# Flamingo block, 64 batches on one core: the move of the scaled rows into the float32r tile goes in two transfers instead of one

## The reference

```python
q = layernorm(x) @ W.T + b
p = softmax(q @ ctx.T + (1 - mask) * -1e9)
x = x + tanh(g_xattn) * (p @ ctx)
x = x + tanh(g_ffn) * (layernorm(x) @ sign(weight).T)
```

## Time and profile before

| | |
|---|---|
| median of three runs | 277.24 us |
| the profiled execution | 277.72 us |
| its span in the trace | 275.9 us |
| TensorE matmul busy | 269.5 us, 98% of the span |
| TensorE weight load busy | 259.0 us |
| VectorE busy | 243.7 us |
| ScalarE busy | 239.7 us |
| GpSimd busy | 178.9 us |
| granted TensorE clock | 1.00 |
| moved by DMA | 64.51 MB in 62754 packets |

### The profile page before, as it was taken

The page is one execution under the profiler, slowest core; times in us unless marked ns, Lnnn a source line. Parts: engine busy times, 40 slices in busy tenths (PEclk is TensorE's granted clock), DMA queues, the critical chain, the costliest instruction groups (busy, mean ns, idle before and its releaser), DMA issues.

```text
span 275.9 us, 9092 instructions
## 1 busy us (share of the span) xinstructions
PE 269.5 (98%) x2215; PEld 259.0 (94%) x2215; DVE 243.7 (88%) x756; ACT 239.7 (87%) x708; POOL 178.9 (65%) x462
## 2 busy tenths in 40 slices
PE   7999999999999999999999999999999999999994
PEld 6899999999999999999999999999999999999983
DVE  2799989999999999999999999999999999998694
ACT  3579899899999999999999999999999999999752
POOL 2387676676677667667666766766676676666553
PEclk9999999999999999999999999999999999999999
DMA  5984797878788787878878877777877877775322
GB/s 147 287 204 122 229 278 236 259 237 284 232 272 255 246 267 241 263 243 266 259 238 274 245 252 254 261 257 233 280 243 249 262 259 251 235 254 175 114 78 114
DMA packets 62754, 64.51 MB, mean 234 GB/s; under 512 B 25425, under 2 KB 38801, under 8 KB 62737
## 3 DMA queue, kind: packets, MB, share of 16 engines
q1 hardware_dynamic: 62016, 63.79, 74.2%
q10 hardware_dynamic: 720, 0.53, 0.7%
HBM read 32.31 MB, written 16.78 MB: 178 GB/s over the span
## 4 chain that ended last, share of the span: by engine, by line
PE 91%; DMA 3%; POOL 1%; ACT 1%; DVE 1%; issue 1%; SPq 1%; POOLq 0%; ACTq 0%
PE ffn_ps L891 21%; PE pv_ps L884 19%; PE l_ps L946 16%; PE ctx_ps L811 11%; PE x1t_ps L952 10%; PE xt_ps L838 6%; PE pt_ps L875 6%; DMA x_in<-in_x_dram 3%; POOL rstd L330 1%; DVE st L597 0%; PE xt_ps L841 0%; PE l_ps L986 0%; DVE xs L617 0%; POOLq L45 0%; SPq L235 0%
## 5 line engine op out<-in xcount | busy, mean ns | idle before, releaser
L946 PE MATMUL l_ps<-m_sb,x_t 128*128 128x77 f32 x488 | 74.1, 254 | 0.1
L946 PEld LDWEIGHTS l_ps<-m_sb,x_t 128*128 128x128 f32 x488 | 71.5, 191 | 0.3 <-issue 0.3
L330 POOL TENSOR_TENSOR rstd<-ve,minus_half 128x4 f32<-128x4 f32 (+1 forms) x70 | 67.4, 963 | 5.5
L952 PE MATMUL x1t_ps<-ident,x 128*128 128x128 f32 x244 | 66.5, 273 | 0.0
L884 PE MATMUL pv_ps<-ctx_v,p_t 77*128 77x256 f32 x252 | 64.8, 379 | 0.0
L448 ACT ACTIVATE xs<-x_in,shift,rstd 128x256 f32<-128x256 f32 x118 | 63.8, 591 | 0.0
L326 POOL TENSOR_TENSOR ve<-st,eps 128x4 f32<-128x4 f32 (+1 forms) x70 | 14.1, 201 | 73.5 <-DVE st L597 73.3
L678 DVE SCALAR_TENSOR_TENSOR x<-pv_ps,recip,x_in 128x256 f32<-128x256 f32 x126 | 54.6, 475 | 0.4 <-PE pv_ps L884 0.3
L597 DVE BATCH_NORM_STATS2 st<-x_in 128x6 f32<-128x512 f32 x64 | 44.0, 687 | 5.3 <-DMA x_in<-in_x_dram 5.3
L386 POOL TENSOR_TENSOR y<-ffn_scaled,x 128x256 f32<-128x256 f32 x63 | 46.3, 735 | 3.2 <-ACT ffn_scaled L515 2.0
L597 DVE BATCH_NORM_STATS2 st<-x 128x6 f32<-128x512 f32 x64 | 43.9, 686 | 3.2
(11 more groups left out here) (100 smaller groups left out, 440.0 us busy)
## 6 DMA issues: line engine op xcount, KB each, us to landing
x_in<-in_x_dram SPq DMA_DIRECT2D x64, 256.0 KB, 2.8
out_dram<-y SPq DMA_DIRECT2D x63, 256.0 KB, 2.4
xs_r<-xs SPq DMA_DIRECT2D x58, 256.0 KB, 2.3
ctx_v<-in_ctx_dram SPq DMA_DIRECT2D x32, 154.0 KB
mask_in<-in_mask_BxSxS_ik_dram SPq DMA_DIRECT2D x32, 154.0 KB, 2.9
ctx_sq<-in_ctx_dram SPq DMA_DIRECT2D x120, 40.0 KB, 2.6
wq_raw<-in_L_xattn_W_dram ACTq DMA_DIRECT2D x1, 256.0 KB, 4.2
wf_raw<-in_L_ffn_weight_dram SPq DMA_DIRECT2D x1, 256.0 KB, 8.4
```

What stands on the lines that cost most here:

```text
L330: pool.tensor_tensor(rstd[:, i, kinds], ve[:, i, kinds], minus_half[:, kinds], ALU.pow).then_inc(rstd_done, 1)
L946: ins = pe.matmul(l_ps[:, j * K:(j + 1) * K], x_t[:, r % 2, c, j * P:(j + 1) * P], m_sb[:, c, r % R], start=(c == 0), stop=(c == C - 1))
L952: ins = pe.transpose(x1t_ps[:, c, j * P:(j + 1) * P], x1[:, (r - 2) % R, j, c * P:(c + 1) * P], ident[:])
```

## The change

`move_xs` issues two DMAs in place of one: row j = 0 of every partition behind `xs0_done`, then row j = 1 behind `xs1_done`. Each copies 1 KB in each of the 128 partitions. Both raise the same semaphore by 16, so the value that TensorE waits for grows by 32 from one use of a buffer to the next, and `moved` says so.

```diff
         def moved(t0, n):
 
-            return t0 * (DMA // 2) + DMA * ((n - MOVE_FIRST) // 2 + 1)
+            return t0 * DMA + T * DMA * ((n - MOVE_FIRST) // 2 + 1)
...
                 i = n % 2
 
-                sp.wait_ge(xs0_done, t0 + n + 1)
-                sp.wait_ge(xs1_done, t0 + n + 1)
-                sp.dma_start(xs_r[:, i].bitcast(F32), xs[:, n % R]).then_inc(xs_moved[i], DMA)
+                for j, done in enumerate((xs0_done, xs1_done)):
+                    sp.wait_ge(done, t0 + n + 1)
+                    sp.dma_start(xs_r[:, i, j].bitcast(F32), xs[:, n % R, j]).then_inc(xs_moved[i], DMA)
```

## The result

The changed kernel takes 280.41 us (median of 4 runs, 278.55 to 281.22) where the kernel before takes 277.12 us in the same runs (276.27 to 277.54). The ratio is 1.0114, with a 95% interval from 1.0082 to 1.0145. The forecast, 277.2 us and no change, was wrong, and so was the range up to 278.2. Now and then one execution of a kernel is over 1.5% slower than its fellows; the ratios in this document leave such executions out, while the medians beside them take in every run. The profiled execution took 280.59 us with a span of 278.8 us, 2.9 us more than before.

What follows compares the result with a forecast made beforehand. TensorE was taken as the bound, busy 269.5 of 275.9 us. 277.72 - 0.16 (a long slot gained) + 0.1 (SP's lateness) gave 277.7 us for the profiled execution, 277.2 us on the median; range 276.4 to 278.2 us.

Steps and rivals of the forecast that it cites:

- TensorE is the bound, and the change can act through its waits for moves alone: Whole kernel: TensorE busy 269.5 of 275.9 us; only its waits for moves can change, 0.80 us in all to gain.
- The first half goes in SP's pause, the second when the whole went: SP's waits before the move: first half issued 0.54 us earlier, second half when the whole is issued now.
- The issues on SP: SP's queue: one more issue per move at 0.52 us, filling 3.71 of 4.04 us a slot, hidden beside TensorE.
- the next slots, with 0.33 us to spare: SP after a turn's last slot: second half 0.1 to 0.3 us late there, taken back in the following slots.
- The transfer: DMA engines: second half lands about 0.3 us sooner, splitting adds 0.9 us of engine time a move; brings nothing.
- The late landings: Five long slots: landings between 0.3 us less and 0.1 us more; only 0.16 us taken as gained.
- the 0.1 us set for SP's lateness: SP after a stall: next one or two halves go later than moves do now, counted as 0.1 us lost.
- The rule: DMA engines shared by both halves: the split brings nothing and costs an issue, sum at zero or just above.
- The slower rival: SP's queue runs out of time, second halves miss their use after stalls: 277.8 to 278.4 us, chance 0.23.
- The faster rival: Late landings absorbed by the halves' lead, all five TensorE waits go: 276.4 us, chance 0.20.

## Why the prediction was wrong

*TensorE is the bound, and the change can act through its waits for moves alone:* right. Its busy time is the same, and its waits for moves went from 0.4 to 3.3 us, where the span grew by 2.9.

*The first half goes in SP's pause, the second when the whole went:* wrong for nearly all slots. It holds where SP has a pause, and SP has one in 7 slots. But the lead is worth something: with both waits first the kernel is about 3 us slower still.

*The issues on SP:* this step failed, in two of its terms. The price of the added issue was taken as 0.52 us and is 0.64, because the second of the two takes 0.59. And the room was taken from one slot, the one at 123.17 us, as 0.33 us. It should have been summed over the turn. From the start of a move to the end of the last issue the eight slots of the turn from 78.77 us take 3.23, 3.25, 3.26, 3.18, 3.23, 3.19, 3.32 and 3.60 us in the trace of before, 26.3 us. Eight times 0.64 us more make 31.4 of the turn's 32.3 us. And SP has pauses that are no waiting. At the end of a turn the trace of before has 0.43 us of them (from 110.63 to 111.06), in a slot where both rows were ready. The changed kernel, always late there, has the same pause:

```profile
141.25 0.85 SPq L251 DMA_DIRECT2D ctx_sq<-in_ctx_dram  x2
142.58 1.12 SPq L260 DMA_DIRECT2D xs_r<-xs  x2
```

That pause of 0.48 us, one of 0.11 and six of 0.05 make 0.9 us in a turn. So 31.4 and 0.9 us fill the 32.3 us, and nothing was free where the prediction had 0.33 us a slot. The words that lateness is taken back by "the next slots, with 0.33 us to spare" are contradicted by the 40 moves of batches 18 to 57, each of which ends 1.1 to 2.2 us after its row: SP gains some 0.1 us a slot within a turn and loses it again at the turn's end.

*The transfer:* right in its direction. Second halves land sooner, 2.1 us against 2.3, though not by 0.3 us. The engines' busy time is unchanged (73.4% of 278.8 against 74.2% of 275.9 us), so splitting a packet of 2 KB costs them nothing that shows.

*The late landings:* right that the lead would not help there, as the packet holds both halves. Too small in size, the second term that failed: the longest landing grew from 3.6 to 4.6 us, where the bound was 0.1 us more, and against the 0.1 us set for SP's lateness the long slots grew by 2.7 us, of which the longer landings are about half. Why they are longer, no run shows.

*The rule* of the Trainium skill, page "DMA: Bandwidth & Descriptors", section "Rules for kernel authors", is that two transfers to disjoint partition halves serialize and one should be used. It gave the right side for these halves by row. For halves by partition, which it names, the run agrees and shows a price: 5.9%, with 2.7 us for a half to land. That the two serialize, no run here shows by itself.

*The slower rival* came nearest: its place (SP's queue) and its point (second halves about 1 us late after a stall) are what the profile shows, though not the longer landings. Its price, 277.8 to 278.4 us, came from the same 0.33 us and so was too low by 2 us, and its chance of 0.23 was low for a queue that the prediction itself filled to 92%.

*The faster rival* fell: long slots stayed, and grew.

## What to carry to other kernels

Issuing a DMA cost SP 0.3 to 0.6 us here, and 4 bytes a partition as much as 2 KB. So before adding one, sum that queue's work over a whole turn of the loop, the dear slots with the cheap ones and the pauses that are no waiting, and compare it with the turn's length. A queue that is idle for 20% of a slot looks free, and the waiting it shows is what absorbs the next stall; 0.4 us of it could go for a loss of 0.2% here, and 0.6 us not. If a wait sits between two pieces of work, an early first piece is worth having only while the queue reaches it early.

## What the runs showed of the hardware that was not expected

An issue of 4 bytes for each of 128 partitions holds SP for 0.47 us, as long as 2 KB for each, and a 256 KB move issued 0.05 us behind it takes 0.59 us. A wait of SP on a semaphore that has its value costs about 0.03 us (0.38 us for 12, 0.62 for 20). The end of a turn of the loop costs SP a pause of 0.43 to 0.48 us. Two transfers of 64 partitions took 2.7 us each to land where two of 128 partitions with the same bytes took 2.1, and the DMA engines were busy for 24 us more over the run (229 against 205). An instruction packet of 16 KB kept one DMA engine for 1.23 us before the change; in the changed kernel, in the window from 61 to 62 us, it took 11.1% of 16 engines, 1.78 us:

```profile
q8 instruction: 1, 0.02, 11.1%
```
